# Attention loop and opening of a fused gated cross-attention and routed feed-forward kernel: values ahead of the transposed scores, and another way of filling the helper rows

## The reference, cut to what is computed

```python
# x (32, 128, 128), ctx (32, 77, 128); 16 heads of 8; 15 routed experts of 256, top 3; shared expert of 512
x = x + tanh(g_xattn) * Attention(layernorm(x), ctx, ctx, w_q, w_k, w_v, w_o)
h = layernorm(x)
weights = softmax(h @ gW + gb); topv, topi = top_k(weights, 3)
router  = sum over the 3 chosen experts of topv * (gelu(h @ rW1[e] + rb1[e]) @ rW2[e] + rb2[e])
x = x + tanh(g_ffn) * (shared_expert(h) + router + h)
```

## Time and profile before

| what | value |
|---|---|
| median of 3 runs | 503.03 us (500.92 to 503.83) |
| profiled execution, its own time | 499.99 us |
| span of its instructions | 498.2 us |
| granted TensorE clock, mean | 0.917 of full speed |
| PE busy | 391.1 us (79%) |
| DVE busy | 306.4 us (62%) |
| ACT busy | 277.0 us (56%) |
| POOL busy | 231.0 us (46%) |

### The profile page before, as it was taken

How to read it: one execution, slowest core, us unless ns; L and a number is a source line. 1 busy time by engine, 2 the same in 40 slices (tenths; PEclk the granted TensorE clock), 3 DMA queues, 4 the chain that set the end, 5 groups by cost and what they waited for, 6 DMA issues and landing times.

```text
span 498.2 us, 11929 instructions
## 1 busy us (share of the span) xinstructions
PE 391.1 (79%) x3870; PEld 349.5 (70%) x3870; DVE 306.4 (62%) x1015; ACT 277.0 (56%) x612; POOL 231.0 (46%) x238
## 2 busy tenths in 40 slices
PE   4586989897989898877887999898999999991000
PEld 2374868676868687767887988788989899991000
DVE  2634567868687777855565778576666546643231
ACT  4355778787778868765464555555555564430000
POOL 6601131267476557534233453044445345557772
PEclk9758899999999999997989999999999999996555
DMA  7589566273535354524567998888989513222221
GB/s 175 163 231 243 138 158 125 105 198 117 150 124 154 109 145 139 158 91 132 137 173 223 284 320 252 222 259 239 270 262 270 167 31 82 59 62 73 74 73 47
DMA packets 69014, 80.11 MB, mean 161 GB/s; under 512 B 10265, under 2 KB 60185, under 8 KB 68953
## 3 DMA queue, kind: packets, MB, share of 16 engines
q1 hardware_dynamic: 60120, 63.08, 45.3%
q0 software_dynamic: 6672, 14.30, 9.7%
q10 hardware_dynamic: 2160, 1.97, 1.2%
HBM read 48.02 MB, written 29.29 MB: 155 GB/s over the span
## 4 chain that ended last, share of the span: by engine, by line
PE 48%; DMA 10%; ACT 10%; DVE 8%; issue 8%; POOL 7%; SPq 5%; DVEq 1%; ACTq 1%; POOLq 0%
PE psum L1364 8%; PE psum L1249 5%; PE psum L1232 5%; PE psum L1475 5%; POOL k_heads L585 4%; PE psum L1354 3%; DMA k_split<-k_parts 2%; DMA xnT<-in_packs 2%; PE psum L1355 2%; PE psum L1356 2%; PE psum L1344 2%; PE psum L1267 2%; POOL q_stack L585 2%; ACT q_stack L647 2%; ACT probs L655 2%
## 5 line engine op out<-in xcount | busy, mean ns | idle before, releaser
L528 POOL DMA_INDIRECT rows_by_expert<-xn_all,row_of x96 | 94.1, 980 | 83.7 <-ACT q_parts L725 45.3
L655 ACT ACTIVATE probs<-psum 77x512 f32<-77x512 f32 x128 | 68.8, 587 | 20.4 <-PE psum L1232 19.0
L585 POOL DMA_INDIRECT k_heads<-outs_by_block,back_row x60 | 56.9, 948 | 45.7 <-PE psum L1475 17.1
L1232 PE MATMUL psum<-q_stack,k_heads 128*77 128x128 f32 x512 | 50.4, 244 | 17.1 <-ACT q_stack L647 17.0
L1232 PEld LDWEIGHTS psum<-q_stack,k_heads 128*77 128x77 f32 x512 | 46.0, 158 | 24.0 <-ACT q_stack L647 23.3
L830 DVE TENSOR_REDUCE max_cols<-psum 128x4 fp32r<-128x312 f32 x128 | 55.3, 474 | 10.6 <-PE psum L1209 10.5
L1354 PE MATMUL psum<-q_parts,w_ring 128*128 128x256 f32 x152 | 50.0, 329 | 13.9 <-ACT probs L733 11.9
L961 DVE CAST w_ring<-w 128x512 fp32r x76 | 38.9, 512 | 29.9 <-issue 21.5
L725 ACT ACTIVATE q_parts<-psum 128x256 fp32r<-128x256 f32 x76 | 29.1, 384 | 34.2 <-PE psum L1344 26.3
L952 DVE TENSOR_TENSOR q_parts<-psum,q_parts 128x256 fp32r<-128x256 f32 x76 | 32.0, 422 | 26.1 <-ACT q_parts L725 25.0
L1354 PEld LDWEIGHTS psum<-q_parts,w_ring 128*128 128x128 f32 x152 | 29.5, 194 | 19.8 <-issue 15.4
(11 more groups left out here) (168 smaller groups left out, 950.3 us busy)
## 6 DMA issues: line engine op xcount, KB each, us to landing
w_raw<-rows_by_expert SPq DMA_DIRECT2D x76, 128.0 KB
outs_by_block<-probs SPq DMA_DIRECT2D x76, 128.0 KB, 3.6
q_stack<-q_split SPq DMA_DIRECT2D x21, 256.0 KB
q_split<-q_parts SPq DMA_DIRECT2D x8, 512.0 KB
k_heads<-k_split SPq DMA_DIRECT2D x96, 39.0 KB
xn<-in_packs SPq DMA_DIRECT2D x19, 193.0 KB
xnT<-in_packs SPq DMA_DIRECT2D x19, 193.0 KB, 3.7
k_parts<-in_packs SPq DMA_DIRECT2D x19, 193.0 KB
```

The costliest lines, as they stand in the source:

```text
L528: nc.gpsimd.indirect_dma_start(xd[:, :], bass.IndirectOffsetOnAxis(ap=row_of[:, r, m:m + 1], axis=0), xn2_all[:, r * GB + m // K, :], None ...
L585: nc.gpsimd.indirect_dma_start(back[j][:, m, :], None, yd[half][:, :], bass.IndirectOffsetOnAxis(ap=back_row[:, j, b * K + k:b * K + k + 1 ...
L655: nc.scalar.activation(probs[0:KV, n % 2, hg * 512:(hg + 1) * 512], st_ps[hg % 2][0:KV, :], ACT.Exp, scale=SCALE).then_inc(exp_done, 1)
L1232: ins = nc.tensor.matmul(st_ps[hg % 2][0:KV, hh * S:(hh + 1) * S], k_heads[:, g % 2, hg, hh, b, 0:KV], q_stack[:, g % 2, hg, b * S:(b + 1) ...
```

## The change

1. **Loop, PE:** `values(t-1)`, with the two routing waits that go with it, moves from behind `scores_t(t, 0)` and `scores_t(t, 1)` to ahead of them. `front_x` and the table step go behind the two.
2. **Loop, ACT:** `oT_leaves(t-1)` moves ahead of `exps(t, 0)`, `xT_leaves` behind `exps(t, 1)`.
3. **Loop, DVE:** `add_base_row(g-2)` moves ahead of `stats1_of(g+3)` and `var1_of(g+3)`.
4. **Helper rows:** POOL zeroes all 128 partitions of `k_heads` and rows 96 to 127 of `q_stack` (one new instruction); SP moves 4 rows of `picks` instead of 32. `zero_q` of groups 0 and 1 is gone.
5. **Opening, queues:** `send_q(0)` is issued by ACT, behind `lead_k(1)`, after a wait for `trail_q(0)`. The last four of the 12 `load_k(0)` are issued by POOL. SP: `send_k(0)` now comes first, and `load_x(2)`, `load_ctx(2)`, `load_x(3)`, the loads of `w_raw` and of group 1 change places. DVE's zeroing of `v_pad` goes behind `trail_k(1)`.

```diff
-            sp.wait_ge(zeroed, 3)
-            zero_q(0, q_zero_in)
+            send_k(0)
+            sp.wait_ge(k_zeroed, 1)
             load_picks(0)
-            send_k(0)
-            load_x(2)
-            load_k(0, 0, 8)
-            send_q(0)
-            load_k(0, 8, 12)
+            load_k(0, 0, 2 * HQ)
             for b in range(GB):
                 first_q(b)
+            load_x(2)
+            load_ctx(2)
+            sp.wait_ge(k_zeroed, 2)
             load_picks(1)
-            load_x(3)
             send_k(1)
             send_q(1)
+            load_k(1, 0, 3 * HQ)
+            load_q(1)
+            load_x(3)
             for p in range(2):
                 load_w1(p)
-            load_k(1, 0, 12)
-            load_q(1)
-            load_ctx(2)
...
-            pool.memset(k_heads[0:KS, 0, 0:2].bitcast(F32), 0.0)
+            pool.memset(k_heads[:, 0, 0:2].bitcast(F32), 0.0)
             pow1(0)
-            pool.memset(k_heads[0:KS, 0, 2:HG].bitcast(F32), 0.0).then_inc(k_zeroed, 1)
+            pool.memset(k_heads[:, 0, 2:HG].bitcast(F32), 0.0).then_inc(k_zeroed, 1)
             pow1(1)
+            pool.wait_ge(k_sent, 16)
+            pool.wait_ge(k_zeroed, 1)
+            for hh in range(HQ):
+                pool.dma_start(k_heads[2 * GR + hh * DK:2 * GR + (hh + 1) * DK, 0, :, hh].bitcast(F32).rearrange("p g b k -> p g (b k)"),
+                               kd[0].rearrange("(g h p) m c -> m h p g c", g=HG, h=HQ)[1, hh]).then_inc(k0_rest_in, 16)
             pool.wait_ge(ln1_rstd, 2)
+            pool.memset(q_stack[KS:P].bitcast(F32), 0.0).then_inc(q_zeroed, 1)
...
             lead_k(1)
+            act.wait_ge(q_lo_ready, 1)
+            act.dma_start(qd[0], q_parts[:].bitcast(F32)).then_inc(q_sent, 16)
             apply1(1, 0, GB)
...
-                if o == 1 and ahead:
-                    xT_leaves(g + 2)
-                exps(t, 0)
-                exps(t, 1)
-                if t >= 1:
-                    oT_leaves(t - 1)
+                if t >= 1:
+                    oT_leaves(t - 1)
+                exps(t, 0)
+                exps(t, 1)
+                if o == 1 and ahead:
+                    xT_leaves(g + 2)
...
+                if t >= 1:
+                    values(t - 1)
+                scores_t(t, 0)
+                scores_t(t, 1)
                 if o == 1 and ahead:
                     front_x(g + 2)
...
-                scores_t(t, 0)
-                scores_t(t, 1)
...
-                if t >= 1:
-                    values(t - 1)
```

More of the change, by code:

```diff
@@ L201, in flamingo_kernel @@
         q0_in = [sem(f"q0_{b}_in") for b in range(GB)]
-        q_zero_in = sem("q_zero_in")
+        q_zeroed = sem("q_zeroed")
+        k0_rest_in = sem("k0_rest_in")
         q_sent = sem("q_sent")
@@ L311, in flamingo_kernel, with k_loaded, q_loaded @@
         table_ps = psum[:, 5, 384:512]
-        def loads_of(g):
-            return g // 2 + g % 2
+        def k_loaded(g):
+            return (g // 2 + 1) * KIN - (HQ * 16 if g % 2 == 0 else 0)
+        def q_loaded(g):
+            return (g // 2 + g % 2) * QIN - 16 * (g % 2)
         @block.sync
@@ L328, in send_k @@
                 if g >= 2:
-                    sp.wait_ge(k_in[g % 2], g // 2 * KIN)
+                    sp.wait_ge(k_in[g % 2], k_loaded(g - 2))
+                if g == 2:
+                    sp.wait_ge(k0_rest_in, HQ * 16)
                 sp.dma_start(kd[g % 2], k_parts[:].bitcast(F32)).then_inc(k_sent, 16)
             def load_k(g, first, end):
-                if first == 0:
-                    if g >= 2:
-                        sp.wait_ge(st_done, (g - 1) * GB * HG)
-                    else:
-                        sp.wait_ge(k_zeroed, g + 1)
-                    sp.wait_ge(k_sent, (g + 1) * 16)
+                if g >= 2:
+                    sp.wait_ge(st_done, (g - 1) * GB * HG)
+                sp.wait_ge(k_sent, (g + 1) * 16)
                 for n in range(first, end):
@@ L366, in load_q @@
                     sp.wait_ge(st_done, (g - 1) * GB * HG)
-                zero_q(g, q_in[g % 2])
+                if g >= 2:
+                    zero_q(g, q_in[g % 2])
                 sp.wait_ge(q_sent, (g + 1) * 16)
@@ L977, in _ @@
             trail_q(0)
+            trail_k(1)
             nc.vector.memset(v_pad[:], 0.0).then_inc(v_zeroed, 1)
-            trail_k(1)
             dve.wait_ge(v_zeroed, 1)
@@ L1031, in _ @@
                     trail_x2(g - 1)
+                if o == 2 and g >= 2:
+                    add_base_row(g - 2)
                 if o == 2 and g + 3 < NG:
@@ L1038, in _ @@
                     add_bias(g - 2)
-                if o == 2 and g >= 2:
-                    add_base_row(g - 2)
                 if t in (TABLE_AT, TABLE_AT + 1):
@@ L1201, in scores @@
                     else:
-                        pe.wait_ge(q_in[g % 2], loads_of(g) * QIN)
+                        pe.wait_ge(q_in[g % 2], q_loaded(g))
                 if b == 0 and hg == 0:
-                    pe.wait_ge(k_in[g % 2], (g // 2 + 1) * KIN)
+                    pe.wait_ge(k_in[g % 2], k_loaded(g))
+                    if g == 0:
+                        pe.wait_ge(k0_rest_in, HQ * 16)
                 if g == 0 and hg == 0:
@@ L1376, in _ @@
                     turn_on(t - 2)
+                if o == 1 and g >= 2:
+                    pe.wait_ge(route_step, (g - 2) * ROUTE + 1)
+                if o == 3 and g >= 2:
+                    pe.wait_ge(route_step, (g - 2) * ROUTE + 12)
+                if t >= 1:
+                    values(t - 1)
+                scores_t(t, 0)
+                scores_t(t, 1)
                 if o == 1 and ahead:
@@ L1382, in _ @@
                     table(0, (t - TABLE_AT) * 2)
-                scores_t(t, 0)
-                scores_t(t, 1)
-                if o == 1 and g >= 2:
-                    pe.wait_ge(route_step, (g - 2) * ROUTE + 1)
-                if o == 3 and g >= 2:
-                    pe.wait_ge(route_step, (g - 2) * ROUTE + 12)
-                if t >= 1:
-                    values(t - 1)
                 if t >= 2:
@@ L1519 @@
     heads = np.arange(4)[None]
-    data["picks"] = np.repeat(-1.0 * (rows[:32, None] == heads), 4 * ctx.shape[1], axis=1).astype(np.float32)
+    data["picks"] = np.repeat(-1.0 * (rows[:4, None] == heads), 4 * ctx.shape[1], axis=1).astype(np.float32)
     data["gW"] = np.concatenate([data["gW"], np.zeros((d, 1), np.float32)], axis=1)
```

18 lines of the change are left out of this document (9 added, 9 removed).

## The result

| what | before | after |
|---|---|---|
| median | 503.29 us (500.92 to 503.83, 4 runs) | 488.76 us (487.74 to 489.62, 4 runs) |
| ratio | | 0.971, interval 0.969 to 0.974 |
| profiled execution, own time (span) | 499.99 (498.2) us | 487.74 (485.8) us |
| start of `turn_max(0)`, of t = 4, of t = 31 | 26.40, 54.24, 211.32 us | 30.47, 49.16, 197.06 us |

What follows compares the result with a forecast made beforehand. PE works most in the loop, idling 17.0 us for turned maxima. Opening and turns 0-3 -2.1, first turns -4.6, fourth -1.7, t = 15 -1.7, small waits -0.6, cover +0.9: -9.8, so 493.0 us; range 486.5 to 500.5.

Steps and rivals of the forecast that it cites:

- The late start: Opening: `load_x(2)` behind the 12 `first_q` makes DVE wait, so `turn_max(0)` starts 4.3 us later, at 30.7.
- `ctx_buf` gone: Turn t = 2: PE's wait for `ctx_buf` of group 2 disappears, 3.3 us gone.
- t = 3 ran at 1.2 GHz: Turn t = 3: slow clock behind the `ctx_buf` standstill; without it the length of t = 4, 2.0 us gone.
- Rival C: Opening: `x_all` lands 5.7 us after issue and the low clock reaches t = 2 and 3; 497.2 us, chance 0.11.
- First turns: First turns of six groups from t = 8: `values` fills PE's waits for the turned maxima, -4.6 us.
- A: Loop: waits only change their names, as DVE or ACT ends first turns too; 498 us, chance 0.14.
- D: Third turns gain as well because DVE's queue is filled earlier, up to 4 us more; 489 us, chance 0.12.
- t = 15: Turn t = 15: `values` fills the ACT wait, `add_base_row` precedes the slow instruction, clock may hold; -1.7 us.
- Fourth turns: Fourth turns: routing ones -0.3 us as DVE is nearly full, t = 7, 27 and 31 -1.4; together -1.7 us.
- Lost cover: Loop: `values` no longer covers the exponentials between the `scores_t` pairs; 0.03 us on each of 28 turns, +0.9 us.
- Rival B: ACT and PE: exponentials lose their cover to `oT_leaves` ahead, 0.5 us a turn, slower; 506 us, chance 0.05.
- Rival E: Loop: `values` finds the last exponentials of t-1 unfinished and waits in the old place; 499 us, chance 0.08.

Runs made afterwards that it cites:

- The opening alone: The changed kernel with the old order of PE, ACT and DVE in the loop: 498.17 us, ratio 0.996.
- `load_x(2)` early: The changed kernel with `load_x(2)` moved ahead of `load_k(0)` and `first_q`: 488.50 us, ratio 0.973.
- the gates moved: The changed kernel with group g+3's statistics spread over first and second turns and gate operations moved from third to fourth turns: 508.49 us, ratio 0.991, third chip.
- the context load alone: The kernel before with `load_ctx(2)` moved ahead of `load_x(3)`: 500.05 us, ratio 0.995.

## Why the prediction was right, and where it was not

The sign, the range and most terms held; the sum was 4.7 us too small on the medians. Up to t = 31 the profiles give 14.3 us where 9.8 were summed: 2.1 are the clock in t = 1, 0.9 the cover that was charged, the rest small terms.

**The late start: right.** `turn_max(0)` forecast at 30.7, measured 30.47, by the chain that was named: SP at `load_x(2)` at 23.02 (22.4), landed 2.7 us later (3.5), DVE idle for it. POOL's chain ended at 25.1 (26.5), each memset of 4096 elements 3.51 us as sized from the earlier trace rows.

**`ctx_buf` gone, `values` filling t = 2: right**, 4.15 us against 3.3 + 0.6.

**The clock of the first turns: mis-sized, by 2.1 us.** The term "t = 3 ran at 1.2 GHz", 2.0 us, held (2.51); what was missing beside it is t = 1, by the belief that a granted 1.00 would come "from about 41 us on". I had let the low stretch move with the loop's start, 10.3 us behind `turn_max(0)`. It began at 25.4 us, while PE stood ahead of the loop, and ended at 35.7 us, 1.2 us earlier than before (36.9), though the loop started 4.07 us later. So t = 1 ran mostly at 2.4 GHz and took 5.06 us, not 7.69; 0.5 had been counted. The opening alone shows the same end, at 35.8 with t = 1 at 5.69: 2.0 us are the clock, 0.6 the order. Rival C had the sign of this wrong: a late start let the low stretch pass in part unused.

The Trainium skill (TensorE: Matmul & The Clock Gate, "HAM oscillation — how this bites in real kernels") says that a wait for data can put TensorE back to its half rate; the prediction read this as a charge for a longer standstill ahead of the loop. Here 7.4 us of standstill cost next to nothing: t = 0 and 1 took 9.12 us together, before it was 11.61, and with `load_x(2)` early, without the standstill, 8.61. The charge did come in `load_x(2)` early, where 5.01 us of waiting in t = 3 were followed by 0.50 again.

**First turns: right**, -4.29 against -4.6. **Second and third turns: right**, unchanged; PE's wait for the residual grew in them from 1.4 to 5.2 us as its wait of 5.1 us went. That DVE's chain sets third turns is shown by the gates moved: 0.34 us less in t = 10. Rivals A and D fall with these. A's price was added up wrongly too: by its own terms, t = 15 and half of the rest, it is 497, not 498.

**Fourth turns: the number right (-1.83 against -1.7) by luck, the reason not.** The routing turns t = 11, 19 and 23 gave 0.93 us where 0.3 was counted, t = 7 and 27 gave 0.90 where 1.4 was counted with t = 31; the two misses cancel. "Leaves DVE's sum the same: -0.3" took DVE as the limit of t = 11. Taking 1.3 us of work off DVE changed nothing there (5.00), and leaving `rank` late cost 1.38. The limit of that turn is PE's order and its wait for `rank`, and edit 3 is needed once `values` stands ahead.

**t = 15: -1.95 against -1.7, for a partly other reason.** In the opening alone and in the context load alone it took 6.37 and 6.32 us with the old order, at a granted 1.00 from 120 to 128 us in both. About 0.45 us belong to the change; the other 1.5 were a clock drop in the profiled execution of before, which isn't always there.

**Lost cover, +0.9: not there.** The four first turns whose wait was 0.6 to 0.7 us got 0.63 or 0.64 us shorter, so nothing was charged beside it, and with `oT_leaves` back behind the exponentials odd turns get longer, not shorter. Rival B had the sign wrong as well. Rival E falls with the 0.7 us left of 17.0.

**Small turns:** t = 4, 25 and 29 gave 0.79 against 0.6; t = 5 gave 0.38 and t = 30 took 0.22, both unforeseen. The 1.9 us given back behind t = 31 were not forecast either; the median's gain is 14.5 all the same.

**Group 0's keys: mis-sized, without effect.** They were taken at 3.1 us to land and in memory at 12.2; issued at 8.73 with no picks ahead, they stood there at 10.91, 2.2 us later. The queries took 4.2 us where 3.1 were taken, so that SP began the `first_q` at 17.44 against 16.9. That the picks ahead of group 1's keys would make them take 6.3 us (issued 25.84, `load_k(1)` at 32.13) was not seen. It cost nothing here, and made the step that would have used the earlier start worthless.

## What to carry to other kernels

Put work that waits for nothing between a request and its answer, and size the gain by turn classes: where another engine's chain ends the turn, the wait only changes its name. An earlier load or start is worth what the next late arrival leaves of it, so follow the queue to the next consumer before counting it. Measure on more than one chip before a gain of 3% is believed: here it was 2.9% on one and 0.4%, not told from none, on another.
